# A two-level channel attention in f32: the symmetric Gram blocks computed once, the value bias moved to TensorE, and a copy on ScalarE moved up

## What is computed

```python
# layer 0: x and ctx, weights 128 x 128, 8 heads of 16 channels
attn = softmax(einsum('bhni,bhnj->bhij', q, k) * scale)
out  = einsum('bhnd,bhde->bhne', v, attn)
res_p2r = xca(heads(rgb, wq_rgb), heads(geo, wk_point), heads(geo, wv_point)) @ proj_p2r.T
res_r2p = xca(heads(geo, wq_point), heads(rgb, wk_rgb), heads(rgb, wv_rgb)) @ proj_r2p.T
x1 = (rgb + res_p2r).T + (geo + res_r2p).T
# layer 1: q and k from ctx, v from x1, each with a bias
scores = einsum('bhdl,bhel->bhde', q, k) / sqrt(128)
o = Wo @ (softmax(scores) @ v) + bo + x1
# then a normalisation over all channels and positions of a batch, with gn_w and gn_b
```

## Time and profile before

| | us |
|---|---|
| median of 3 runs | 328.22 |
| lowest, highest | 326.43, 331.25 |
| the profiled execution's own time | 328.15 |
| its span, first to last instruction | 326.3 |
| PE, weight loads, DVE, ACT, POOL busy | 307.2, 269.2, 261.7, 233.1, 190.1 |

### The profile page before, as it was taken

One profiled execution on the slowest core, in us unless ns is written; L12 is line 12 of the kernel. 1 busy time (PEld: TensorE's weight loads), 2 busy tenths in 40 slices (PEclk: granted clock), 3 DMA queues, 4 the chain that ended last, 5 costly groups with the idle time before them and its releaser, 6 DMA issues.

```text
span 326.3 us, 12574 instructions
## 1 busy us (share of the span) xinstructions
PE 307.2 (94%) x4792; PEld 269.2 (82%) x4792; DVE 261.7 (80%) x707; ACT 233.1 (71%) x385; POOL 190.1 (58%) x277
## 2 busy tenths in 40 slices
PE   6999958999997899999999999999999999999990
PEld 4887857898986689898988989898988889898760
DVE  2495874988898498888889888888889898876883
ACT  2664734887878379787878779787878779787575
POOL 0874481675656647575766757575766746575611
PEclk9999999999999999999999999999999999999997
DMA  7999999179798985979899897979799895220036
GB/s 230 378 250 273 256 292 262 24 262 278 197 294 217 292 210 147 311 216 289 227 300 249 241 304 193 310 200 298 221 298 249 248 266 152 106 109 20 2 129 257
DMA packets 39060, 73.87 MB, mean 226 GB/s; under 512 B 4608, under 2 KB 26368, under 8 KB 39040
## 3 DMA queue, kind: packets, MB, share of 16 engines
q1 hardware_dynamic: 35008, 58.92, 66.7%
q10 hardware_dynamic: 4032, 14.68, 12.9%
HBM read 56.81 MB, written 16.78 MB: 226 GB/s over the span
## 4 chain that ended last, share of the span: by engine, by line
PE 91%; issue 3%; DVE 2%; DMA 1%; ACT 1%; SPq 0%; POOLq 0%; POOL 0%
PE oacc L427 10%; PE oacc L434 9%; PE oacc L428 8%; PE mid L530 4%; PE gacc L387 4%; PE mid L507 4%; PE mid L454 4%; PE stat L389 4%; PE tpx L344 4%; PE gacc L388 3%; PE gacc L389 3%; PE stat L387 3%; PE stat L388 3%; PE mid L516 2%; PE gacc L405 2%
## 5 line engine op out<-in xcount | busy, mean ns | idle before, releaser
L1135 POOL TENSOR_TENSOR xy_lo<-raw,xy_hi 128x256 fp32r<-128x256 f32 x256 | 179.5, 738 | 119.8 <-ACT xy_hi L704 119.8
L704 ACT ACTIVATE xy_hi<-raw 128x1024 fp32r<-128x1024 f32 x64 | 67.0, 1048 | 0.0
L866 DVE STREAM_TRANSPOSE t<-y_blocks 128x512 f32<-128x512 f32 x56 | 62.4, 1158 | 0.0
L711 ACT ACTIVATE res<-oacc 128x512 f32<-128x512 f32 x59 | 34.9, 593 | 29.0 <-PE oacc L434 28.7
L895 DVE BATCH_NORM_STATS2 hstat<-res 128x6 f32<-128x512 f32 x60 | 40.1, 687 | 15.5 <-ACT res L711 15.4
L427 PE MATMUL oacc<-xy_hi,pq_hi 128*128 128x512 f32 x120 | 52.4, 436 | 0.1
L428 PE MATMUL oacc<-xy_lo,pq_hi 128*128 128x512 f32 x120 | 47.4, 395 | 1.6 <-issue 1.6
L387 PE MATMUL gacc<-t 128*32 128x129 f32 x224 | 43.1, 273 | 2.6 <-issue 2.6
L390 PE MATMUL gacc<-t 128*32 128x225 f32 x224 | 45.4, 354 | 0.0
L389 PE MATMUL gacc<-t 128*32 128x225 f32 x224 | 45.4, 354 | 0.0
L390 PE MATMUL stat<-t 128*32 128x225 f32 x224 | 45.1, 353 | 0.0
(11 more groups left out here) (166 smaller groups left out, 905.3 us busy)
## 6 DMA issues: line engine op xcount, KB each, us to landing
raw<-in_x SPq DMA_DIRECT2D x31, 512.0 KB, 5.8
raw<-in_ctx SPq DMA_DIRECT2D x31, 512.0 KB, 6.9
y_blocks<-in_ctx SPq DMA_DIRECT2D x112, 128.0 KB, 7.0
out<-res ACTq DMA_DIRECT2D x28, 512.0 KB, 3.5
x_blocks<-in_x SPq DMA_DIRECT2D x56, 128.0 KB, 6.9
out<-res SPq DMA_DIRECT2D x4, 512.0 KB, 2.7
wt<-in_weights SPq DMA_DIRECT2D x1, 896.0 KB, 6.8
raw<-in_x SPq DMA_DIRECT2D x2, 256.0 KB, 3.8
```

The source lines that it names most:

```text
L704: act.activation(xy_hi[slot][:, s, :], raw[slot][:, s, :], ACT.Copy).then_inc(split_hi, 1)
L866: dve.transpose(dst, blocks[:, HC * i:HC * (i + 1)]).then_inc(yt_ready, 1)
L1135: piece = pool.tensor_tensor(xy_lo[slot][:, s, cols], raw[slot][:, s, cols], xy_hi[slot][:, s, cols].bitcast(f32), ALU.subtract)
```

## The change

It has four parts.

1. The Gram's blocks against y are computed once each: ten of sixteen. In batch 0 strip 0 takes columns 64 to 256 and 0 to 31, strip 1 96 to 256 and 0 to 63, strip 2 128 to 256 and 32 to 95, strip 3 64 to 256. In batch 1 strip 0 takes 96 to 256 and 0 to 31, strip 1 128 to 256 and 0 to 63, strip 2 128 to 256 and 0 to 95, strip 3 32 to 256. So the strips stream 225, 225, 193, 193 columns in batch 0 and 193, 193, 225, 225 in batch 1: over the pair 418 each instead of 450. There are seven matmuls a chunk instead of six. Strips 2 and 3 of a chunk are issued before 0 and 1, and from the end of batch 0 on they are one chunk ahead in the program.
2. The mirror on DVE takes eight transposes: four of both batches, and two more for each batch alone.
3. The value bias is applied as two matmuls of one column, z times `bv` for each batch, with a copy of the vectors whose halves are swapped (`vec_rot`, two more loads). Three DVE operations of `softmax_out` go, and the wait for them. The copies of z, the m products and `c_out` stay.
4. `split_high` of batch 0 of the next pair, x part, moves on ACT from behind the second normalisation to the place before `norm_scale`.

The waits: both halves' operand waits of the Gram and the wait for `var_ready` keep their place before the first matmul of batch 1, which now comes before the last chunk of strips 0 and 1 of batch 0. The wait for `attn` stands before the last two chunks of strips 0 and 1 of batch 1.

```diff
-            def gram_chunks(h, u, b, begin, end):
...
+            def strip(u, b, c, j, columns):
+                tb, acc = t[2 * u + b], gacc_b[b]
+                rows = slice(W32 * j, W32 * (j + 1))
+                for k, (begin, end) in enumerate(columns):
+                    mm = pe.matmul(acc[rows, begin:end], tb[:, c, rows], tb[:, c, begin:end],
+                                   start=(c == 0 and k == 0), stop=(c == CH - 1 and k == len(columns) - 1))
+                return mm
+            def upper_strips(u, b, c):
+                if b == 0:
+                    strip(u, b, c, 0, ((H64, GW), (0, W32)))
+                    return strip(u, b, c, 1, ((3 * W32, GW), (0, H64)))
+                strip(u, b, c, 0, ((3 * W32, GW), (0, W32)))
+                return strip(u, b, c, 1, ((C, GW), (0, H64)))
+            def lower_strips(u, b, c):
+                if b == 0:
+                    strip(u, b, c, 2, ((C, GW), (W32, 3 * W32)))
+                    strip(u, b, c, 3, ((H64, GW),))
+                else:
+                    strip(u, b, c, 2, ((C, GW), (0, 3 * W32)))
+                    strip(u, b, c, 3, ((W32, GW),))
+            def gram_pair(h, u, post, p):
+                for c in range(CH - 1):
+                    if c % HC == 0:
+                        gram_operands(h, u, 0, c // HC)
+                    lower_strips(u, 0, c)
+                    upper_strips(u, 0, c)
+                lower_strips(u, 0, CH - 1)
+                gram_operands(h, u, 1, 0)
+                if post:
+                    pe.wait_ge(var_ready, p - 2)
+                lower_strips(u, 1, 0)
+                upper_strips(u, 0, CH - 1).then_inc(gram_done, 1)
+                for c in range(1, CH):
+                    if c == HC:
+                        gram_operands(h, u, 1, 1)
+                    lower_strips(u, 1, c)
+                    if c == CH - 1:
+                        z_operands(p - 1)
+                    upper_strips(u, 1, c - 1)
+                upper_strips(u, 1, CH - 1).then_inc(gram_done, 1)
...
+            sp.dma_start(vec_rot[0:H64, :], vectors[H64:C, :]).then_inc(weights_in, 16)
+            sp.dma_start(vec_rot[H64:C, :], vectors[0:H64, :]).then_inc(weights_in, 16)
...
-                pe.wait_ge(abv_ready, p + 1)
-                pe.matmul(mid0[:, 2 * C:2 * C + 2], w("oT"), abv[:, :], start=True, stop=True)\
-                    .then_inc(wo_abv_done, 1)
+                for a in range(2):
+                    mm = pe.matmul(mid0[:, 2 * C + a:2 * C + a + 1], z[:, a, 2, :], (col("bv"), col("bv", vec_rot))[a],
+                                   start=True, stop=True)
+                mm.then_inc(wo_bv_done, 1)
...
-                for i, j in ((0, 3), (1, 0), (2, 0), (3, 2)):
+                for i, j, bs in ((3, 0, BOTH), (0, 1, BOTH), (1, 2, BOTH), (2, 3, BOTH), (2, 0, 0), (3, 1, 0), (0, 2, 1), (1, 3, 1)):
                     rows, cols = slice(W32 * i, W32 * (i + 1)), slice(W32 * j, W32 * (j + 1))
-                    last = dve.transpose(gram[rows, :, cols], gram[cols, :, rows])
+                    last = dve.transpose(gram[rows, bs, cols], gram[cols, bs, rows])
...
+                    split_high(h, u, 0, 0, back)
                     if post:
                         norm_scale(p - 3)
                         normalise(*before(h, u), 0)
```

More of the change, by code:

```diff
@@ L56, in cross_attention_pair_kernel @@
         quad = sb("quad", [C, 2, W32])
-        bk32, bv32 = quad[:, 0, :], quad[:, 1, :]
+        bk32 = quad[:, 0, :]
+        vec_rot = sb("vec_rot", [C, len(VNAMES)])
         cst = sb("cst", [C, 2 * C + W32 + 6])
@@ L67, in w, with col @@
             return wt[:, WNAMES.index(name), :]
-        def col(name):
+        def col(name, table=vec):
             k = VNAMES.index(name)
-            return vec[:, k:k + 1]
+            return table[:, k:k + 1]
         nbq = sb("nbq", [C, 1])
@@ L126, in cross_attention_pair_kernel @@
         probs = [bank[:, k:k + 6 * W32].rearrange("p (i c) -> p i c", c=W32) for bank, k in ((mid0, 6 * W32), (tail[0], 0))]
-        abv_s = [bank[:, 12 * W32:12 * W32 + 2] for bank in (mid0, tail[0])]
         o_next = [oacc, [gacc, oacc[0]]]
@@ L173, in cross_attention_pair_kernel @@
         m3_done = sem("m3_done")
-        wo_abv_done = sem("wo_abv_done")
+        wo_bv_done = sem("wo_bv_done")
         n_ready = sem("n_ready")
@@ L372, in y_transpose_early @@
                 mm.then_inc(y_early_done, 1)
-            def gram_chunks(h, u, b, begin, end):
[L376 to L382, removed]
-                    pe.wait_ge(gram_ready, n - 1)
[L384 to L394, removed]
@@ new lines, in gram_operands @@
+            def gram_operands(h, u, b, half):
+                n = 4 * h + 2 * u + b
+                pe.wait_ge(xt_ready[b], 2 * (2 * h + u) + half + 1)
+                pe.wait_ge(yt_ready, 2 * n + half + 1)
+                if half == 0:
+                    pe.wait_ge(gram_ready, n - 1)
+            def strip(u, b, c, j, columns):
[5 more added lines that the diff above has]
+                return mm
@@ L579, in step @@
                     scores(p - 1)
-                    gram_chunks(h, u, 0, 0, 4)
-                    gram_chunks(h, u, 0, 4, 8)
-                    if post:
-                        pe.wait_ge(var_ready, p - 2)
-                    gram_chunks(h, u, 1, 0, 4)
-                    gram_chunks(h, u, 1, 4, 7)
-                    z_operands(p - 1)
-                    gram_chunks(h, u, 1, 7, 8)
+                    gram_pair(h, u, post, p)
                     z_products(p - 1)
@@ L641, in keys_times_sums @@
                 if isinstance(p, int) and p < 1:
[L642 removed]
+                    act.wait_ge(weights_in, 112)
                 else:
@@ L775, in step @@
                         normalise(*before(h, u), 1)
-                    split_high(h, u, 0, 0, back)
                     if post:
@@ L998, in softmax_out @@
                                   own_half[:, :].unsqueeze(1).broadcast_to([C, 6, 2]), ALU.mult).then_inc(inv2_ready, 1)
-                dve.wait_ge(abv_step, 2 * p + 2)
-                dve.tensor_tensor(abv[:, :], abv_s[last][:, :], sinv[:, 4:6], ALU.mult).then_inc(abv_ready, 1)
                 if not (isinstance(p, int) and p < 1):
```

19 lines of the change are left out of this document (5 added, 14 removed).

## The result

The changed kernel takes 336.60 us (median of 4 runs, 335.53 to 341.46). The kernel before, run beside it, took 327.39 (326.43 to 331.25). The ratio is 1.025 with an interval of 1.016 to 1.034. So it is slower, and its median lies outside the range of the prediction (325.8 to 333.8); whether it is slower by more than 2% the interval leaves open. The profiled execution of after is its longest, 341.46, with a span of 339.7.

A forecast was written before the change was run, and what follows sets the result against it. PE bounds the loop, DVE's chain 0.17 us shorter; the bound moves to DVE. On 328.15 us: twelve steps +1.6, two -0.3, prologue +1.0, bias at ends +0.4, tail -0.1, together +2.6, 330.7; said 330.5, range 325.8 to 333.8.

The forecast's parts named there:

- PE's own work: TensorE's own time in one loop step: 18.35 us before, forecast 18.22 after the shorter Gram and the value bias.
- DVE's sum of +0.30 for `nmat`: In a loop step, nmat later by mirror 0.7 minus softmax 0.12 minus idle gap 0.28, against a slack of 0.17.
- The Gram (-0.35 a step): On PE, strips stream 418 columns instead of 450; gain between 0.28 and 0.44 us a step, 0.35 taken.
- rival 2: Strips on PE cannot run a chunk ahead, so the Gram keeps its length; step 18.57, total 332.5 us, chance 0.1.
- The value bias (+0.22): On PE, two one-column matmuls replace one of two columns, four weight-loading passes for two: +0.22 us a step.
- The mirror (+0.7): On DVE, four new 32x32 transposes at about 0.17 to 0.18 us each, together +0.7; bounds 0 and 1.0.
- The softmax (-0.12): On DVE, three operations go from softmax_out, so the attention starts 0.12 us earlier (0 to 0.42).
- "Cost nothing" for the moved high part: On ACT, split_high (1.05 us) fills the idle 1.17 before norm_scale; GpSimd's work comes 2.5 us sooner; no cost.
- The idle gap of 0.28 that goes: On DVE, the 0.28 us idle before the next statistic vanishes because ACT delivers earlier.
- the waits for the attention and the bias: PE's moved attention wait costs 0 to 0.1 us inside its spare time; n3_out's wait for the bias costs nothing.
- The prologue (+1.0, and 0.22 for the bias): At the start, +0.7 us for the first mirror and 0.3 for two more weight loads; bias 0.22 in the first step.
- rival 4: One more PE "issue" stop from code loading, as PE's program grows: +1.7 to +2.9 us, total 333, chance 0.09.

The follow-up runs named there:

- e8: e6 with the Gram matmuls of both batches sorted by the time each strip would reach them; 330.77 us, ratio 1.010.
- e9: e8 with the value bias back on DVE as before, without the vec_rot loads; 327.73 us, ratio 1.004.
- e10: The changed kernel with the reciprocal of the softmax sum written to PSUM instead of SBUF; 330.19 us, ratio 1.012.
- e5: The changed kernel with the Gram and the four-transpose mirror of before; value bias on PE and moved high part stay; 335.80 us, ratio 1.027.
- e7: The kernel before with one edit alone, the high part of batch 0 moved up on ACT before norm_scale; 329.58 us, ratio 1.002.
- e3: The changed kernel, strips on lines of their own, with the attention wait moved back to the last Gram matmul; 334.69 us, ratio 1.022.
- e2: The changed kernel, strips on lines of their own, without the four one-batch mirror transposes (four Gram blocks unfilled); 333.96 us, ratio 1.031.
- e4: e3 and e2 together: late attention wait and no one-batch mirror transposes, against the changed kernel; 335.41 us, ratio 1.036.
- e6: The changed kernel, strips on lines of their own, with the exponential ahead of the first normalisation on ACT; 333.19 us, ratio 1.023.

## Why the prediction was wrong

Two steps of the prediction failed. The first is PE's own work: "PE's own step becomes 18.35 - 0.35 + 0.22 = 18.22". It is 18.63, because the Gram did not get shorter. The second is DVE's sum of +0.30 for `nmat`, which is +0.59, because the mirror was under-sized and the softmax gave nothing. The second sets the step of after; the first alone would have made it 18.63 in place of 18.48.

The frame was right. PE's work and DVE's chain stand side by side, the slack between them is 0.17, and the bound moves to DVE. With the measured +0.59 in place of my +0.30 the same sum gives 18.35 - 0.17 + 0.59 = 18.77, and the step is 18.70 to 18.77. But with PE at 18.63 DVE decides by 0.10 us only, where I had 0.26.

- **The Gram (-0.35 a step): wrong, and rival 2 was nearly the mechanism.** I had given it 0.10, because L389 at 161.15 ahead of L387 at 161.17 seemed to show strips that don't wait for each other, and had left open whether a drift of 0.44 is possible. The drift of 0.35 does come, but the strips must also catch up, and there the order of the program binds. The Gram stays at 6.30, the length that I had worked out for strict program order and set aside. e8 shows that the size of the gain (0.36 of my 0.28 to 0.44) was right, for an order of issue that the change does not have.
- **The value bias (+0.22): right**, 0.24 between e8 and e9 and 0.23 by the rows of after (0.92 against 0.69).
- **The mirror (+0.7): under-sized.** Eight transposes take 1.86, +0.87. A 32x32 takes 203 ns against 238 for the double, where I had some 0.17 us: most of the time of a small transpose does not depend on its elements, which a slope drawn from a large one hides. The upper bound held.
- **The softmax (-0.12): it gave nothing.** The attention starts 0.97 after the sum's start; before, 0.95. The three operations went, but the halved reciprocal grew from 0.16 to 0.24 and now starts behind an exposed reciprocal.
- **"Cost nothing" for the moved high part: wrong.** "GpSimd gets its work 2.5 us sooner, which nobody waits for" looked only at who waits for its result. The price is paid by DVE, which worked beside it. In after it is 0.07 a step for the held operation (0.24 against e10's 0.17); in e5 and e7, with the old Gram, it is 1.6 us in four and two of the steps, and in e3, with the new Gram, 1.35 in one.
- **The idle gap of 0.28 that goes, the waits for the attention and the bias, ACT's gain: right.** ACT's wait fell to 0.23, forecast 0.2.
- **The prologue (+1.0, and 0.22 for the bias): +2.1 in after.** The mirror is +0.87 of it, fully on the path, and the bias +0.23 (14.02 us from the mirror's end to the first load, 13.79 in the kernel before). The rest, 1.05, is that the mirror starts at 19.61 instead of 18.56. That is not the two weight loads, since e5 and e2 have them and start it at 18.31 and 18.51; its start varies between 18.1 and 20.4 over these profiles, and why it does is open.
- **Code loading (rival 4, +1.7 to +2.9):** the stops are larger and vary more than a rival with one price can say: two executions of the same instructions differ by 10 us. It also left out that the clock can fall behind a stop, 3.0 us in after's profile.

In the sum, the median of 336.60 is 6.1 us over my 330.5. Steps of 18.48 became 18.73: that is 3 us of the miss, the prologue one more, and the rest, some 2 us, is not told apart by any run; the first four steps, which vary by up to 10 us, are where it can lie.

## What to carry to other kernels

When work is divided evenly over parallel strips of PE, write the matmuls in the order in which the strips will reach them: here a strip got 0.35 us ahead and no more, and the same matmuls took 6.30 or 5.94 us by order alone. When an operation is moved, ask not only who waits for it but what it will now run beside: here GpSimd moved over a DVE operation with two inputs in SBUF cost that operation up to 2.1 us, and one input in PSUM removed it. A kernel whose start is noisy by several us is compared step by step, by one event per step, and not by its total.

## What the runs showed of the hardware that was not expected

- A strip's pass on PE may start ahead of older passes of other strips, of nine at most in e4's Gram, where L412's last chunks lead by 0.31 us; beyond that it starts when they do (0.01 behind). The Trainium skill (TensorE: Matmul & The Clock Gate, Part 3, What overlaps and what doesn't) has matmuls start and end in program order; e4's rows disagree on the starts up to this lead (L412's eighth chunk at 143.53, L390's seventh, which stands ahead of it in the program, at 143.81 and 143.84) and agree beyond it (144.65 behind 144.64).
- A DVE operation of 12 elements was held 2.27 us, through several GpSimd operations one behind the other. The same operation took 0.24 in after, 0.43 to 0.62 in the loop of e9 (early exponential), and 2.3 in some steps of e3, e5 and e7. The profiles show what sets the length. In the eleven kernels with the reciprocal in SBUF it took 0.19 us or more 145 times, and each time it ended 0.02 to 0.03 us after a GpSimd operation's end. So it depends on how long before that end it comes. In e6, for one (DVE, then GpSimd), it ends at 163.97 and GpSimd's piece at 163.94:

```profile
163.52 0.45 DVE L1031 TENSOR_TENSOR sinv<-sinv,own_half 128x12 f32<-128x12 f32 x1
```
```profile
163.19 0.75 POOL L1167 TENSOR_TENSOR xy_lo<-raw,xy_hi 128x256 fp32r<-128x256 f32 x1
```

  In 138 of the 145 it was the first or second such end after the operation's start. In the seven long cases it was the end of GpSimd's whole run; why it was not let in at an earlier one is open.
- Two executions with the same instructions had 88.90 and 78.88 us in the same four first steps, in stops of PE's weight loads of up to 4.3 us and a clock at 1.2 GHz behind one of them:

```profile
PEld oacc L459 <- issue: 6.5, 14, 4.3
```
